# Attention scores from two rounded 32-bit parts on 64 rows, in two row tiles of TensorE side by side, in place of three bf16 parts on 96 rows

## The chip, the cores and the metric

The kernel runs on one core of a Trainium2 chip. A core has TensorE (PE, matmuls into PSUM), VectorE (DVE), ScalarE (ACT), GpSimd (POOL) and SyncE (SP), each with its own queue of instructions, and 16 DMA engines that move data between HBM and the on-chip SBUF. The metric is the device time of one execution in microseconds. Before the change three runs gave 1751.22 to 1751.84 us, with a median of 1751.62 us.

## The reference

The input is x of shape (2, 2048, 256). One transformer layer is computed:

```python
x = x + layernorm(attn(layernorm(x)))
x = x + layernorm(ffn(layernorm(x)))
```

The attention has 16 heads of 16 columns, so with 2 batches there are 32 head units. Its keys and values come from a latent of 64 columns:

```python
q = x @ W_q
latent = (x @ W_k + x @ W_v) @ W_down_kv
k_rec, v_rec = latent @ W_up_k, latent @ W_up_v          # per head
scores = einsum('bhqd,bhkd->bhqk', qh, k_rec) / sqrt(256)
scores = scores * exp(-0.01 * |t_q - t_k|)               # decay, 2048 x 2048
out = softmax(scores) @ v_rec                            # then @ W_o
```

The ffn has 2 shared and 16 routed experts, of which each token uses the best 2. Everything is float32.

## The kernel before, in words

**Stages.** A prologue (`prologue`) normalises x in 8 blocks of 512 tokens, forms the values of all heads, and prepares queries and keys of the first 8 heads of both batches. Then `attention` goes through 32 heads. The ffn follows block by block and is not touched.

**How scores are made.** The decay splits into a factor of the query's place times a factor of the key's place, in two variants (falling, rising) on the two sides of the diagonal. So `prepare` multiplies a projected chunk by both factors. To multiply at float32 accuracy with bf16 operands it splits each product into three bf16 parts (L229 to L235 in the prologue, L527 to L536 in the attention): round, subtract, round the rest, subtract. `store_parts` writes the parts to DRAM (L108). `load_stack` (L111) then gathers, for one head, 96 rows (6 combinations of parts times 16 head columns) for each of four kinds: QL, QU, KL, KU. It issues 12 DMAs for a head: per kind one of 48 rows, one of 32 and one of 16, each row 2048 bf16 numbers or 4 KB. For the queries the 48 and the 32 rows are copies of one part, by a source that repeats (`to_broadcast`). `stack` has two buffers (`par`).

**A head.** It has 16 steps, one for each tile of 128 keys. In step s TensorE makes the scores of 128 keys against 2048 queries in two halves of 1024 (`scores`, L604), each half in 2 or 3 matmuls; ACT takes the exponential of each half in one instruction of 128x1024 (L683); before that DVE multiplies the 128x128 block on the diagonal by a mask (`mask`, L511), which lies in half 0 for s below 8 and in half 1 after that. TensorE then multiplies the probabilities of step s-2 by the values (`products`, L613), four 512-column chunks in four column tiles, in float32. PSUM has three slots of one half each: half h needs the exponential of half h-3 to be done (`halves_done`). In the row of a step the queue of TensorE holds: scores of half 0, products of step s-2, scores of half 1.

**What else rides along.** In the first head of each of the first 12 pairs TensorE projects one chunk of queries and one of keys for later heads (L597, after steps 7 and 11), and DVE prepares them. At step 4 TensorE transposes the sums of the head before (L620).

**The queue of SP.** All DMAs are issued by SP, in program order. While head n runs, SP waits until the scores of head n-1 are done (`sc_ps`), and issues the load of head n+1 into the buffer that became free. In the first head of a pair it then stores the attention output of the pair before (L436), and in the second head, ahead of the load, the four DMAs of freshly prepared parts (L108). Where a load crosses to the next 8 heads it waits until those stores have landed (`out0`, `out1`). TensorE waits at the start of a head for its load (`stk0`, `stk1`).

Of the kernel before, what the change touches and what calls it, by code (L numbers as in the profile page):

```python
# [5 lines left out]
F32 = mybir.dt.float32  # L6
U32 = mybir.dt.uint32
I32 = mybir.dt.int32
BF16 = mybir.dt.bfloat16
ALU = mybir.AluOpType  # L10
# [4 lines left out]
P = 128  # L15
# [20 lines left out]
STACK_DMAS = 12  # L36
BF16_ONES = float(np.array([0x3F803F80], np.uint32).view(np.float32)[0])
PRIME = 2
FLAGS = 936


def emit(nc, io):
    ctx = ExitStack()
    with ctx:
        sb = lambda n, s, d=F32: ctx.enter_context(nc.sbuf_tensor(n, s, d))
        given = []
        def sem(n):
# [9 lines left out]
        w_unit = sb("w_unit", [P, 2, KD, P])  # L57
        stack = sb("stack", [P, 2, 4, S], BF16)
        part = sb("part", [P, 2, 2, 3, CH], BF16)
        work = sb("work", [P, 17408])  # L60
        ps = ctx.enter_context(nc.psum_tensor("ps", [P, 8, CH], F32))

        dram = lambda n, s: nc.dram_tensor(n, s, F32, kind="Internal").ap()
        attn_dram = dram("attn_dram", [T, D])
        parts_dram = nc.dram_tensor("parts_dram", [4, 3, B * H, HD, S], BF16, kind="Internal").ap()

        common = dict(nc=nc, io=io, sem=sem, ident=ident, xT=xT, V_all=V_all, decay=decay, small=small,
                      w_qk=w_qk, w_unit=w_unit, stack=stack, part=part, work=work, ps=ps,
                      attn_dram=attn_dram, parts_dram=parts_dram)
        prologue(**common, shifted=False)  # L70
# [4 lines left out]
        with nc.If(beyond == 1):  # L75
            nc.all_engine_barrier()
            nc.clear_and_free_semaphores(given)
            nc.all_engine_barrier()
            common["sem"] = lambda n: nc.alloc_semaphore("s_" + n)
            prologue(**common, shifted=True)  # L80
            layer(**common, attend=attention_shifted)
# [38 lines left out]
def prologue(nc, io, sem, ident, xT, V_all, decay, small, w_qk, w_unit, stack, part, work, ps, parts_dram, shifted, **_):  # L120
# [36 lines left out]
    with nc.Block() as block:  # L157
# [33 lines left out]
        def _(pool):  # L191
            nc.gpsimd.memset(mhalf, -0.5).then_inc(half_set, 1)
            pool.wait_ge(half_set, 1)
            for n in range(NB):
# [8 lines left out]
                if shifted and n >= NB - 4:  # L203
# [143 lines left out]


def attention(nc, sem, ident, xT, V_all, decay, small, w_qk, w_unit, stack, part, work, ps, attn_dram, parts_dram, first_block, **_):

    probs = carve(work, 0, 3, S)
    Vg = carve(work, 10240, 2, KT, STRIP)
    O_sb = carve(work, 11264, CH)
    att = carve(work, 11776, KT, 2 * HD)
    split = carve(work, 12288, 2, CH)
    dmask, _ = diagonal_masks(small)
    rden = carve(small, 256, CT, QC)
    bound = carve(small, 928, 2)
    bound_new = carve(small, 930, 2)
    bound_all = carve(small, 932, 2)  # L360
    after_bd = carve(small, 934, 1)
    flags = carve(small, FLAGS, B * H // 2 + 1).bitcast(I32)
    QL, QU, KL, KU = range(4)
    ACC = 6

    names = ("vg w proj_ps proj_free prep_link prep_sb sc_ps masked exp_done pv_done o_sb oT_ps rden_sb att_sb").split()
    s_ = {n: sem("a_" + n) for n in names}
    s_.update(att_out=sem("a_att_out"), stk0=sem("a_stk0"), stk1=sem("a_stk1"), out0=sem("a_out0"), out1=sem("a_out1"))
    vg_set, bd_all, bd_link, flag = sem("vg_set"), sem("a_bd_all"), sem("a_bd_link"), sem("a_flag")
    wait = lambda eng, name, v: eng.wait_ge(s_[name], v + PRIME)  # L370
    prime = lambda eng, *ns: [eng.sem_inc(s_[n], PRIME) for n in ns]

    NSTEP = KT
    HALF = S // 2
    NHALF = 2 * NSTEP
    NPAIR = B * H // 2
    PPU = P // HD // 2
    ROWS = 6 * HD
    SCALE = 1.0 / D ** 0.5
    PREPS = 2 * (NPAIR - PPU)  # L380
    chunk = lambda c: slice(c * CH, (c + 1) * CH)

    def cut(lo, hi):

        while lo < hi:
            end = min(hi, (lo // CH + 1) * CH)
            yield lo, end
            lo = end

    def score_pieces(kt, half):  # L390

        a, z = half * HALF, (half + 1) * HALF
        own = kt * P
        for lo, hi in cut(a, min(z, own)):
            yield lo, hi - lo, QU, KU
        for lo, hi in cut(max(a, own), z):
            yield lo, hi - lo, QL, KL

    def half_of(s, half):

        return 2 * ((2 * s + half) % (ACC // 2))

    def halves_done(n, s, half):

        h = 2 * s + half
        return n * NHALF + (h - 1 if h < 2 else h - 2)

    def probs_of(par, s):

        return (par * NSTEP + s) % 3  # L410

    def tiles_done(par, n, s):

        return n * NSTEP + (s - 1 if par == 0 and s < 2 else s - 2)

    def own_block(s):

        at = s * P % HALF
        bank = half_of(s, s * P // HALF) + at // CH
        return ps[:, bank, at % CH:at % CH + P]  # L420

    def pairs(eng, pair):
        pair(0, True, True, False)
        with eng.Fori(1, NPAIR - PPU) as it:
            pair(it, True, False, False)
        with eng.Fori(NPAIR - PPU, NPAIR - 1) as it:
            pair(it, False, False, False)
        pair(NPAIR - 1, False, False, True)

    with nc.Block() as block:  # L430
        @block.sync
        def _(sp):
            def store_att(it):
# [4 lines left out]
            def pair(it, prep, first, last):  # L438
                for par in range(2):
# [6 lines left out]
                    if not end:  # L446

                        wait(sp, "sc_ps", n * NHALF)
                        if not first or par:
                            for which in range(2):  # L450
                                wait(sp, f"out{which}", (it + par) // PPU * (32 * QC))
# [1229 lines left out]
```

## Time and profile before

| | us |
|---|---|
| median of 3 runs | 1751.62 |
| profiled execution, whole | 1757.73 |
| its span, first to last instruction | 1756.0 |
| prologue and first load (to 118) | 118 |
| 32 heads (118 to 1228) | 1110 |
| ffn (1228 to 1756) | 528 |
| PE busy in the span | 1650.1 (94%) |
| ACT busy in the span | 1163.8 (66%) |
| DVE busy in the span | 613.8 (35%) |
| TensorE's granted clock, mean | 0.977 |

The profile is one execution. Its own time, 1757.73 us, is 1.73 us more than its span and 0.35% over the median of the runs. "Busy" counts the time in which at least one instruction of an engine was under way. For matmuls the end of each is modelled, so a busy PE is not a PE at its peak. SP's rows are the issue of DMAs, not their transfer; how busy the DMA engines are is a column of the stage view.

### The profile page before, as it was taken

How to read it: one execution, taken by the hardware profiler on the slowest of the kernel's cores; microseconds unless marked ns; L12 is line 12 of the kernel's file. 1: busy time of each engine (PE TensorE's matmuls, PEld its weight loads, DVE VectorE, ACT ScalarE, POOL GpSimd, SP SyncE). 2: the span in 40 equal slices, each digit the busy share in tenths (PEclk: the TensorE clock that was granted, in tenths of full speed). 3: DMA queues.
4: the chain of work that ended last, by engine and by line, in shares of the span. 5: the costliest groups of instructions: out<-in, count | busy, mean ns of one | idle time of the engine just before them, and what ended most of it. 6: DMA issues, size and time to landing. Idle time of an engine off the chain costs nothing. (4 is left out here: it accounts for less than half of the span.)

```text
span 1756.0 us, 26320 instructions
## 1 busy us (share of the span) xinstructions
PE 1650.1 (94%) x8752; PEld 646.0 (37%) x8753; DVE 613.8 (35%) x1688; ACT 1163.8 (66%) x1330; POOL 59.9 (3%) x104
## 2 busy tenths in 40 slices
PE   7639999999999999999999999998899999999996
PEld 5502222222222222222222222223465565466454
DVE  5804324234143242341341111112344434534432
ACT  4428898988998987989988999998232232222210
POOL 1000000000000000000000000000000000000000
PEclk9969999999999999999999999999899999999998
DMA  7412122122222221222222111123110000100000
GB/s 193 120 64 72 64 76 78 62 75 74 72 74 65 77 73 59 73 79 72 73 62 81 50 44 58 55 87 78 31 37 24 32 16 24 36 12 24 13 12 14
DMA packets 104017, 104.68 MB, mean 60 GB/s; under 512 B 46576, under 2 KB 91376, under 8 KB 103712
## 3 DMA queue, kind: packets, MB, share of 16 engines
q1 hardware_dynamic: 103968, 104.08, 20.2%
q8 instruction: 24, 0.39, 0.1%
q14 instruction: 25, 0.20, 0.0%
HBM read 70.51 MB, written 33.55 MB: 59 GB/s over the span
## 5 line engine op out<-in xcount | busy, mean ns | idle before, releaser
L683 ACT ACTIVATE work<-ps 128x1024 f32<-128x1024 f32 x1024 | 993.9, 1025 | 139.7 <-DVE ps L511 73.4
L604 PE MATMUL ps<-stack 96*128 96x512 bf16 (+3 forms) x2432 | 552.3, 350 | 56.0 <-POOL work L475 32.1
L613 PE MATMUL ps<-work 128*32 128x512 f32 x4096 | 550.6, 610 | 0.0
L511 DVE TENSOR_TENSOR ps<-ps,small 128x128 f32<-128x128 f32 x512 | 153.1, 299 | 804.9 <-PE ps L604 804.9
L604 PEld LDWEIGHTS ps<-stack 96*128 96x128 bf16 x2432 | 189.4, 98 | 620.8 <-ACT work L683 252.2
L1568 PE MATMUL ps<-xT,stack 128*128 (+1 forms) x320 | 156.4, 612 | 1.5 <-PEq L430 1.5
L613 PEld LDWEIGHTS ps<-work 128*32 128x32 f32 x4096 | 81.3, 108 | 189.1 <-ACT work L683 112.0
L1576 PE MATMUL ps<-xT,stack 128*128 (+1 forms) x320 | 150.4, 592 | 0.0
L1591 PE MATMUL ps<-stack,work 128*128 128x256 f32 x640 | 141.3, 380 | 0.0
L1541 ACT ACTIVATE work<-ps 128x512 f32<-128x512 f32 x80 | 47.6, 595 | 135.5 <-PE ps L1568 135.3
L1591 PEld LDWEIGHTS ps<-stack,work 128*128 128x128 f32 x640 | 120.6, 190 | 15.8 <-issue 0.2
L1629 DVE TENSOR_TENSOR work<-work,ps 128x512 f32<-128x512 f32 x80 | 54.9, 687 | 160.0 <-PE ps L1576 152.3
L1576 PEld LDWEIGHTS ps<-xT,stack 128*128 128x128 f32 x320 | 60.9, 190 | 76.8 <-issue 73.0
L1568 PEld LDWEIGHTS ps<-xT,stack 128*128 128x128 f32 x320 | 56.2, 191 | 50.8 <-issue 49.4
L1292 ACT CAST decay<-ps 48x512 f32 (+1 forms) x8 | 4.6, 578 | 80.0 <-PE ps L1329 80.0
L475 POOL COPY work<-V_all 128x256 f32 (+1 forms) x32 | 14.4, 449 | 1014.8 <-PE ps L613 1014.8
L1633 DVE TENSOR_TENSOR work<-work,ps 128x512 f32<-128x512 f32 x64 | 44.0, 687 | 6.7
L597 PE MATMUL ps<-xT,w_unit 128*128 (+1 forms) x96 | 45.2, 592 | 0.0
L304 PE MATMUL ps<-work,xT 128*128 128x256 f32 x128 | 34.7, 420 | 10.9 <-ACT xT L340 10.9
L1285 ACT COPY part<-ps 128x512 f32<-128x512 f32 x16 | 9.4, 585 | 48.2 <-PE ps L1317 48.2
L345 ACT COPY V_all<-ps 128x256 f32<-128x256 f32 x32 | 10.3, 375 | 38.5 <-PE ps L304 38.5
L304 PEld LDWEIGHTS ps<-work,xT 128*128 128x128 f32 x128 | 25.8, 211 | 18.8 <-ACT xT L340 13.4
(119 smaller groups left out, 806.9 us busy)
## 6 DMA issues: line engine op xcount, KB each, us to landing
parts_dram<-part SPq DMA_DIRECT2D x64, 384.0 KB, 4.0
stack<-parts_dram SPq DMA_DIRECT2D x128, 192.0 KB
stack<-parts_dram SPq DMA_DIRECT2D x128, 128.0 KB
work<-in_L_attn_x SPq DMA_DIRECT2D x16, 512.0 KB, 5.0
stack<-parts_dram SPq DMA_DIRECT2D x128, 64.0 KB
attn_dram<-work SPq DMA_DIRECT2D x16, 256.0 KB, 14.0
work<-attn_dram SPq DMA_DIRECT2D x8, 512.0 KB, 3.9
out<-work SPq DMA_DIRECT2D x8, 512.0 KB, 3.0
```

Of the source, the lines that this page charges most:

```text
L304: m = nc.tensor.matmul(ps[:, 6 + j // 2, (j % 2) * D:(j % 2 + 1) * D], xT[:, k, at:at + P], w_veff[:, k], start=k == 0, stop=k == KD - 1)
L511: nc.vector.tensor_tensor(own_block(s), own_block(s), dmask, ALU.mult).then_inc(s_["masked"], 1)
L597: m = nc.tensor.matmul(ps[:, bank], w_unit[:, which, k], xT[:, k, at:at + CH] if isinstance(at, int) else xT[:, k, bass.ds(at, CH)], start ...
L604: m = nc.tensor.matmul(ps[:, half_of(s, half) + q0 // CH % 2, q0 % CH:q0 % CH + w], stack[0:ROWS, par, k, s * P:(s + 1) * P], stack[0:ROWS ...
L613: m = nc.tensor.matmul(ps[STRIP * c:STRIP * (c + 1), ACC + par], Vg[:, par, s], probs[:, probs_of(par, s), chunk(c)], start=s == 0, stop=s ...
L683: nc.scalar.activation(probs[:, probs_of(par, s), half * HALF:(half + 1) * HALF], src, ACT.Exp, scale=SCALE).then_inc(s_["exp_done"], 1)
L1541: nc.scalar.activation(gate[:, h % 2], ps[:, G + h % 2], ACT.Silu).then_inc(s_["gate_sb"], 1)
L1568: m = nc.tensor.matmul(ps[:, G + h % 2], w_up[:, 0, k, h], x(k), start=k == 0, stop=k == KD - 1)
L1576: m = nc.tensor.matmul(ps[:, U + h % 2], w_up[:, 1, k, h], x(k), start=k == 0, stop=k == KD - 1)
L1591: m = nc.tensor.matmul(ps[:, DOWN + j // 2, (j % 2) * D:(j % 2 + 1) * D], hid[:, h, j * P:(j + 1) * P], w_dn[:, h], start=h == 0, stop=h = ...
L1629: nc.vector.tensor_tensor(hid[:, h], gate[:, h % 2], ps[:, U + h % 2], ALU.mult).then_inc(s_["hu_sb"], 1)
L1633: nc.vector.tensor_tensor(hid[:, h], hid[:, h], ps[:, C], ALU.mult).then_inc(s_["h_sb"], 1)
```

## The change

The three bf16 parts become two parts in a 32-bit format that is rounded when it is written (`float32r`). A head then needs 4 combinations of parts times 16 columns, which is 64 rows. The upper 64 rows of SBUF hold the same keys a second time; with them the lower row tile of TensorE (rows 0 to 63) makes the first 1024 queries and the other (rows 64 to 127) makes the last 1024. So keys lie in 128 rows of 2048 numbers and queries in 128 rows of 1024, for the falling and the rising factor each, in 4 bytes a number. The buffers K_st and Q_st lie over `stack` and `work`. `scores` now makes both halves of a step in one go, ahead of the products, with the matmuls of the two tiles in turn. `prepare` has three pieces in place of five. A load is 16 DMAs. `prologue_shifted`, a copy of the old prologue, serves only the path for large scores, which these inputs do not take.

```diff
+def store_halves(sp, halves_dram, part, rows, c, which, done):
+    cols = chunk_at(c)
+    for a in range(2):
+        dst = halves_dram[2 * which + a].rearrange("i h d s -> i (h d) s")[:, rows, cols]
+        sp.dma_start(dst.rearrange("i r s -> r i s"), part[:, which, a]).then_inc(done, 16)
+
+def load_halves(sp, K_st, Q_st, halves_dram, m, par, done):
+    for a in range(2):
+        keys = halves_dram[2 + a].rearrange("i h d s -> i (h d) s")[:, bass.ds(m * HD, HD)]
+        queries = halves_dram[a].rearrange("i h d s -> i (h d) s")[:, bass.ds(m * HD, HD)]
+        for g in range(2):
+            for i in range(2):
+                at = g * TILE_ROWS + 2 * HD * i
+                src = keys[i:i + 1].to_broadcast([2, HD, S])
+                sp.dma_start(K_st[at:at + 2 * HD, par, a, :].bitcast(F32), src).then_inc(done, 16)
+                src = queries[:, :, g * (S // 2):(g + 1) * (S // 2)]
+                sp.dma_start(Q_st[at:at + 2 * HD, par, a, :].bitcast(F32), src).then_inc(done, 16)
...
             for which in range(2):
                 sp.wait_ge(parts_out[which], 2 * 16 * QC)
-            load_stack(sp, stack, parts_dram, 0, 0, stack_in)
+            sp.wait_ge(xn_ready, NB)
+            load_halves(sp, K_st, Q_st, halves_dram, 0, 0, stack_in)
...
-                nc.vector.tensor_copy(pt[:, :, 0], split).then_inc(prep_link, 1)
-                dve.wait_ge(prep_link, 3 * k + 1)
-                nc.vector.tensor_tensor(split, split, pt[:, :, 0], ALU.subtract).then_inc(prep_link, 1)
-                dve.wait_ge(prep_link, 3 * k + 2)
-                nc.vector.tensor_copy(pt[:, :, 1], split).then_inc(prep_link, 1)
-                dve.wait_ge(prep_link, 3 * k + 3)
-                nc.vector.tensor_tensor(pt[:, :, 2], split, pt[:, :, 1], ALU.subtract).then_inc(prep_sb, 1)
+                nc.vector.tensor_copy(pt[:, :, 0].bitcast(F32R), split).then_inc(prep_link, 1)
+                dve.wait_ge(prep_link, k + 1)
+                nc.vector.tensor_tensor(pt[:, :, 1].bitcast(F32R), split, pt[:, :, 0], ALU.subtract).then_inc(prep_sb, 1)
...
-            def scores(par, n, s, half):
-                wait(pe, "exp_done", halves_done(n, s, half))
-                for q0, w, q, k in score_pieces(s, half):
-                    m = nc.tensor.matmul(ps[:, half_of(s, half) + q0 // CH % 2, q0 % CH:q0 % CH + w],
-                                         stack[0:ROWS, par, k, s * P:(s + 1) * P],
-                                         stack[0:ROWS, par, q, q0:q0 + w], start=True, stop=True)
-                m.then_inc(s_["sc_ps"], 1)
+            def scores(par, n, s):
+
+                wait(pe, "exp_done", halves_done(n, s, 1))
+                halves = [list(score_pieces(s, half)) for half in range(2)]
+
+                late = len(halves[0]) > len(halves[1])
+                order = [(0, 0), (1, 0), (0, 1), (0, 2), (1, 1)] if late else [(half, i) for i in range(3) for half in range(2)]
+                for half, i in order:
+                    if i < len(halves[half]):
+                        q0, w, a = halves[half][i]
+                        tile = slice(half * TILE_ROWS, (half + 1) * TILE_ROWS)
+                        m = nc.tensor.matmul(ps[:, half_of(s, half) + q0 // CH % 2, q0 % CH:q0 % CH + w],
+                                             K_st[tile, par, a, s * P:(s + 1) * P], Q_st[tile, par, a, q0 % HALF:q0 % HALF + w],
+                                             start=True, stop=True)
+                        if i == len(halves[half]) - 1:
+                            m.then_inc(s_["sc_ps"], 1)
...
                     for s in range(NSTEP):
-                        scores(par, n, s, 0)
+                        scores(par, n, s)
                         if s >= 2:
                             products(par, n, s - 2)
                         elif not (first and par == 0):
                             products(1 - par, n - 1, NSTEP - 2 + s)
-                        scores(par, n, s, 1)
```

The queue of SP, the load of one head, before (`stack` is the buffer on chip, `parts_dram` the parts in DRAM; a shape is rows by numbers in a row):

```order
L117 DMA stack<-parts_dram 48x1x2048
L117 ISA
L117 DMA stack<-parts_dram 32x1x2048
L117 ISA
L117 DMA stack<-parts_dram 16x2048
L117 ISA
L117 DMA stack<-parts_dram 48x1x2048
L117 ISA
L117 DMA stack<-parts_dram 32x1x2048
```

and after, at the same place:

```order
L149 DMA K_st<-halves_dram 32x1x2048
L151 REGISTER_ALU
L151 DMA Q_st<-halves_dram 32x1x1024
L149 ISA
L149 DMA K_st<-halves_dram 32x1x2048
L151 DMA Q_st<-halves_dram 32x1x1024
L149 DMA K_st<-halves_dram 32x1x2048
L151 ISA
L151 DMA Q_st<-halves_dram 32x1x1024
```

Four groups of 48, 32 and 16 rows of 2-byte numbers became eight pairs of 32 rows and 32 rows of 4-byte numbers.

The queue of TensorE in two steps of a head, before (`a_exp_done` counts the exponentials; `work` holds probabilities and values):

```order
L604 MATMUL ps<-stack 128x512 [waits a_exp_done]
L604 MATMUL ps<-stack 128x512
L613 MATMUL ps<-work 32x512 [waits a_exp_done]
L613 MATMUL ps<-work 32x512 x3
L370 REGISTER_ALU
L604 MATMUL ps<-stack 128x512 [waits a_exp_done]
L604 MATMUL ps<-stack 128x512
L370 REGISTER_ALU
L604 MATMUL ps<-stack 128x512 [waits a_exp_done]
L604 MATMUL ps<-stack 128x512
```

and after:

```order
L627 MATMUL ps<-Q_st,K_st 128x512 [waits a_exp_done]
L627 MATMUL ps<-Q_st,K_st 128x512
L627 MATMUL ps<-Q_st,K_st 128x128
L627 MATMUL ps<-Q_st,K_st 128x384
L627 MATMUL ps<-Q_st,K_st 128x512
L394 REGISTER_ALU
L637 MATMUL ps<-work 32x512 [waits a_exp_done]
L637 MATMUL ps<-work 32x512 x3
```

The two score groups of a step stand together now, behind one wait, and the products stand behind both.

## Rows read from the trace of the kernel before

**Rows 1.** Stages: start:end, us, busy per engine (x), PEclk, DMA share, GB/s
```profile
0.00:118.00 118.00, 63.04 (x241) 44.61 (x243) 64.08 (x150) 36.17 (x83) 12.49 (x28) 0.86 0.48 131
118.00:1228.00 1110.00, 1081.68 (x6772) 307.83 (x6776) 325.53 (x825) 999.63 (x1036) 23.86 (x48) 0.99 0.24 69
1228.00:1756.00 528.00, 505.39 (x1744) 293.54 (x1736) 224.19 (x713) 127.98 (x211) 23.53 (x29) 0.98 0.07 23
```
**Rows 2.** Timeline, two undisturbed steps: start, us, engine, line, what, count
```profile
603.65 1.07 PE L613 MATMUL ps<-work 128*32 128x512 f32 x8
604.65 1.04 PE L604 MATMUL ps<-stack 96*128 96x512 bf16 x5
605.62 1.06 PE L613 MATMUL ps<-work 128*32 128x512 f32 x8
...
605.70 1.94 ACT L683 ACTIVATE work<-ps 128x1024 f32<-128x1024 f32 x2
...
608.41 1.98 ACT L683 ACTIVATE work<-ps 128x1024 f32<-128x1024 f32 x2
```
**Rows 3.** DMA issues of the page: KB each, us to landing
```profile
parts_dram<-part SPq DMA_DIRECT2D x64, 384.0 KB, 4.0
stack<-parts_dram SPq DMA_DIRECT2D x128, 192.0 KB
stack<-parts_dram SPq DMA_DIRECT2D x128, 128.0 KB
...
stack<-parts_dram SPq DMA_DIRECT2D x128, 64.0 KB
```
**Rows 4.** One load of a head: its issue on SP, then stages of 1 us
```profile
1052.31 11.61 SPq L117 DMA_DIRECT2D stack<-parts_dram  x12
...
1061.00:1062.00 1.00, 1.00 (x9) 0.16 (x10) 0.30 (x1) 1.00 (x2) 0.00 (x0) 1.00 0.20 66
1067.00:1068.00 1.00, 1.00 (x11) 0.20 (x9) 0.30 (x1) 1.00 (x2) 0.00 (x0) 1.00 0.13 53
1075.00:1076.00 1.00, 1.00 (x9) 0.16 (x8) 0.10 (x1) 0.97 (x2) 0.00 (x0) 1.00 0.13 53
1076.00:1077.00 1.00, 1.00 (x9) 0.37 (x5) 0.23 (x1) 1.00 (x2) 0.00 (x0) 1.00 0.06 25
```
**Rows 5.** A head whose load came late, on TensorE and ACT, and a stage behind
```profile
672.29 1.03 PE L604 MATMUL ps<-stack 96*128 96x512 bf16 x2 [3.13 <-DMA stack<-parts_dram]
...
675.26 1.96 ACT L683 ACTIVATE work<-ps 128x1024 f32<-128x1024 f32 x2 [4.71 <-PE ps L613]
...
676.00:678.00 2.00, 2.00 (x12) 0.42 (x10) 0.30 (x1) 1.22 (x2) 0.00 (x0) 0.50 0.30 100
```
**Rows 6.** Stages of 1 us: a store of attention output (1034), a store of parts
```profile
1034.00:1035.00 1.00, 1.00 (x9) 0.45 (x11) 0.12 (x1) 0.97 (x2) 0.00 (x0) 1.00 1.02 201
574.00:575.00 1.00, 1.00 (x9) 0.41 (x5) 0.13 (x1) 0.97 (x2) 0.00 (x0) 1.00 1.00 340
```
**Rows 7.** Prologue, its end: the last prepare on DVE, the first loads, TensorE's start
```profile
82.61 0.69 DVE L233 CAST part<-work 128x1024 bf16<-128x1024 f32 x1
83.34 1.23 DVE L235 TENSOR_TENSOR part<-work,part 128x1024 bf16<-128x1024 f32 x1
...
89.51 1.64 SPq L117 DMA_DIRECT2D stack<-parts_dram  x2
...
115.78 2.66 SPq L117 DMA_DIRECT2D stack<-parts_dram  x4
...
117.96 4.23 PE L604 MATMUL ps<-stack 96*128 96x512 bf16 x12 [32.10 <-POOL work L475]
```
**Rows 8.** Timeline, start of the last head on TensorE
```profile
1182.61 0.59 PE L604 MATMUL ps<-stack 96*128 96x512 bf16 x2 [0.49 <-ACT work L683]
```
**Rows 9.** Timeline, a mask on DVE and the exponential that it releases
```profile
1030.94 0.30 DVE L511 TENSOR_TENSOR ps<-ps,small 128x128 f32<-128x128 f32 x1 [2.11 <-PE ps L604]
...
1031.27 1.02 ACT L683 ACTIVATE work<-ps 128x1024 f32<-128x1024 f32 x1 [0.18 <-DVE ps L511]
```

More of the change, by code:

```diff
@@ L9 @@
 BF16 = mybir.dt.bfloat16
+F32R = mybir.dt.float32r
 ALU = mybir.AluOpType
@@ L36 @@
 STACK_DMAS = 12
+TILE_ROWS = 4 * HD
+HALVES_DMAS = 16
 BF16_ONES = float(np.array([0x3F803F80], np.uint32).view(np.float32)[0])
@@ L39, with aligned @@
 FLAGS = 936
+def aligned(at):
+    return (at + 31) // 32 * 32
 def emit(nc, io):
@@ L57, in emit @@
         w_unit = sb("w_unit", [P, 2, KD, P])
+        stack_at = aligned(nc.sbuf_base)
         stack = sb("stack", [P, 2, 4, S], BF16)
         part = sb("part", [P, 2, 2, 3, CH], BF16)
+        work_at = aligned(nc.sbuf_base)
         work = sb("work", [P, 17408])
+        K_st = nc.alloc_sbuf_tensor_at("K_st", [P, 2, 2, S], F32R, offset=stack_at)
+        Q_st = nc.alloc_sbuf_tensor_at("Q_st", [P, 2, 2, S // 2], F32R, offset=work_at + 4 * 3 * S)
         ps = ctx.enter_context(nc.psum_tensor("ps", [P, 8, CH], F32))
@@ L64, in emit @@
         attn_dram = dram("attn_dram", [T, D])
+        halves_dram = nc.dram_tensor("halves_dram", [4, 2, B * H, HD, S], F32, kind="Internal").ap()
         parts_dram = nc.dram_tensor("parts_dram", [4, 3, B * H, HD, S], BF16, kind="Internal").ap()
@@ L68, in emit @@
                       w_qk=w_qk, w_unit=w_unit, stack=stack, part=part, work=work, ps=ps,
-                      attn_dram=attn_dram, parts_dram=parts_dram)
-        prologue(**common, shifted=False)
+                      attn_dram=attn_dram, parts_dram=parts_dram, halves_dram=halves_dram, K_st=K_st, Q_st=Q_st)
+        prologue(**common)
         layer(**common, attend=attention)
@@ L79, in emit @@
             common["sem"] = lambda n: nc.alloc_semaphore("s_" + n)
-            prologue(**common, shifted=True)
+            prologue_shifted(**common)
             layer(**common, attend=attention_shifted)
@@ L117, in load_stack @@
             sp.dma_start(stack[row * HD:(row + count) * HD, par, kind, :], parts).then_inc(done, 16)
-def prologue(nc, io, sem, ident, xT, V_all, decay, small, w_qk, w_unit, stack, part, work, ps, parts_dram, shifted, **_):
+def store_halves(sp, halves_dram, part, rows, c, which, done):
[3 more added lines that the diff above has]
+        sp.dma_start(dst.rearrange("i r s -> r i s"), part[:, which, a]).then_inc(done, 16)
@@ L122, in prologue, with prologue_shifted @@
+def prologue_shifted(nc, io, sem, ident, xT, V_all, decay, small, w_qk, w_unit, stack, part, work, ps, parts_dram, **_):
     w_k = carve(work, 0, KD, D)
@@ L201, in _ @@
                     nc.gpsimd.tensor_copy(w_unit[:, :, :, :], w_qk[:, :, :, 0:P]).then_inc(w_set, 1)
-                if shifted and n >= NB - 4:
+                if n >= NB - 4:
                     if n == NB - 4:
```

783 lines of the change are left out of this document (486 added, 297 removed).

## The prediction

> **What bounds the kernel now.** I read the stages first, then the timeline of single steps, then the DMA part of the page, and last one load of a head in stages of 1 us. The 32 heads take 1110 of 1756 us, with TensorE busy for 1082 of them; the ffn takes 528 and is left as it is [rows 1]. In an undisturbed step TensorE goes from products (603.65) to scores (604.65) to the next products (605.62): 1.00 + 0.97 = 1.97 us, without a gap. ACT's exponentials start every (608.41 - 605.70) / 3 = 0.90 us there, so its floor is 1.81 us a step [rows 2]. TensorE sets the pace, by 0.16 us a step. That is what one sees first, and it says that cheaper scores can win at most 512 x 0.16 = 82 us.
>
> The column that matters for this change is another one. Over the heads the 16 DMA engines are 0.24 busy [rows 1], which looks like ample room. But the load of one head, issued at 1052.31, still runs at 1076: 24 us for 1.57 MB, out of the 34.6 us that a head takes (1110 / 32). From 1067 on the share is 0.13 at 53 GB/s, and 0.13 x 16 is 2 engines; before that, at 1061, it is 0.20, 3 engines [rows 4]. So the load goes over two or three engines, one after another. The bytes agree. If a DMA of 48 rows is cut over 3 engines, one of 32 rows over 2 and one of 16 rows over 16, and each takes the same first engines, then these carry, of the 192, 128 and 64 KB per kind [rows 3], 64 + 64 + 4 = 132 KB, times four kinds 528 KB, or 541 thousand bytes. At 53 / 2.08 = 25.5 GB/s an engine that is 21 us; seen are 24.2 us from the issue to the end, with about 2 us ahead of the first data. Had each DMA gone to engines of its own, five would have been busy at once.
>
> The Trainium skill, "DMA: Bandwidth & Descriptors", section "Why a DMA increments its semaphore by 16 and not by 1", states this as a rule: a DMA runs on the largest number up to 16 that divides the slowest dimension of both sides, and on the lowest-numbered engines. By that rule the 48-row DMAs (a source that leads with 3) get 3 engines and the 32-row ones (a source that leads with 2) get 2, which the trace bears out, and each of the 16 new DMAs would get 2.
>
> **The change part by part.** *The load.* Every new DMA has 32 rows on chip and a source that leads with 2 (two copies, or two parts), like the old 32-row ones; none is left of 48 or 16 rows. Keys are 128 rows x 2 x 2048 x 4 = 2.10 MB and queries 128 x 2 x 1024 x 4 = 1.05 MB: 3.15 MB in place of 1.57. All of it goes over 2 engines, 1.573 million bytes each, in place of 0.541: 2.9 times as much on the busiest. At the tail's 25.5 GB/s a load takes 61.7 us. At the rate of a whole load of before, 0.541 / 24.2 = 22.3 GB/s with its start counted, 70.4 us. I take 64: back to back there is no start to pay, but at 1061 three engines moved 66 GB/s, only 20.6 each, in the part with repeated sources [rows 4], and keys are such a part.
>
> *Where it lies.* 64 us is longer than a head. Load n+2 may be issued when head n's scores are done, some 35 us after load n landed, while load n+1 still has 29 us to go. So the two engines have the next load queued always, and the period of a head is their load time. Double buffering hides a head behind a load now, not a load behind a head.
>
> *The sum.* Prologue: each of 8 prepares on DVE loses one cast (0.69 us) and one subtraction (1.23) [rows 7], about 15 us if the first copy keeps its 0.69, 11 if it rises to 1.2 by writing four bytes; I take 12. The added wait on xn_ready is for ACT's work that was long done. So the first load is issued at 89.5 - 12 = 77.5. Before, the next load was issued 26.3 us after it (115.78 - 89.51); now 26.3 + (64 - 22.3) = 68 later, at 145.5, with data from 147.5. Then:
> - 31 loads x 64 = 1984;
> - stores of parts in 12 pairs: 4 x 524 KB, 131 KB on each engine, at 340 / 16 = 21 GB/s [rows 6] 6.2 us; before, one landed in 4.0 us [rows 3]; I take 5.5, 66 us in all;
> - 14 stores of attention output ahead of the last load, in pieces of 128 bytes: 16 KB an engine at 201 / 16.3 = 12.3 GB/s [rows 6] is 1.3 us; I take 2.5 for the small pieces, 35 in all (18 to 55);
> - 3 crossings to the next 8 heads, where the load waits for stores to land: 4 us each, 12.
>
> The last load has landed at 147.5 + 1984 + 66 + 35 + 12 = 2244.5. From there on the kernel ends as now: the last head started at 1182.6 [rows 8], 573.4 us before the end of the span. TensorE comes cold out of its wait: after such a wait of 3.13 us the granted clock was 0.50 (1.2 GHz) and still stood there at 676, and ACT had lost 4.7 us by 675.26 [rows 5]; I add 5. Span 2823, execution 2825 with the 1.7 us around it; the median stood 0.35% under the profiled execution, which gives 2815. I forecast 2815.
>
> *Scores and products.* They lie beneath the loads and cost nothing as long as a head stays under 64 us. The exponential (1.02), the scores, the mask (0.30) and some 0.1 of hand-overs [rows 9] form a chain in steps 0 to 7, since half 0 of a step now waits, with half 1 behind the same wait, for the exponential of half 0 of the step before. The trace has no matmul in the rounded format. Lower bound of a score stage: half of today's 0.97, two tiles at bf16's speed, 0.49 us. Upper bound: float32 products take 1.00 us for four chunks side by side [rows 2], so four score matmuls of that price one after another 4.0 us. A head is then 16 x 1.9 = 31 us at the low end and 16 x (4.0 + 1.02 + 0.4) = 87 at the high one; in pairs, 16 x 3.4 = 55. I take the low end, nearest to the bf16 row in work; only the high end would show. The wait for `halves_done(n, s, 1)` at step 0 asks for the last exponential of the head before: about 1.2 us a head, hidden too. If the loads were hidden, all this would count.
>
> *DVE.* Two operations less per prepare, in slack before and after. The store is ready earlier, but queued behind a load.
>
> **The rivals.** A: the new DMAs spread over all engines. For it: stores and ffn weights do (340 GB/s, share 1.00 [rows 6]); at that rate a load takes 9 us. Then heads run at their own pace: steps 0 to 7 at 1.02 + 0.65 + 0.4 = 2.07 us, the others at ACT's 1.81, and 1.2 at the start, 32.3 against 16 x 1.97 = 31.5 now: +26 us; the prologue gives 12 and the late loads [rows 5] some 15. About 1750: this is the side of faster or no change. Against it: 32-row DMAs ran at share 0.13 [rows 4]. The section "Bandwidth" of the same page of the Trainium skill speaks for A, since larger transfers move faster there (64 KB at 138 GB/s, 1 MB at 341), and ours grow from 64 to 192 KB to 128 and 256 KB; but the rows have 53 GB/s for 128 and 192 KB, and the measurement decides.
> B: the scores cost the high end, 87 us a head, and set the pace themselves: 147 + 32 x 87 + 528 = 3460. It decides from 64 us a head, that is a score stage of some 2.6 us. Nothing in the trace speaks for float32's price, since each score is still one matmul in the queue, but a float32 product is one there too and shows as two rows.
> C: the two engines run dry between loads, because SP is held back in its issues (12 took 11.6 us [rows 4]) or by its waits: 4 to 8 us a load more, 2940 to 3060.
>
> **How the numbers follow.** The forecast has 86%; A 4% (half of it faster), B 3%, C 7%. Its own bounds: 61.7 us a load and the low ends of the stores give 2815 - 74 - 35 = 2705, somewhat less if rows of 8 KB run better than those of 4 KB; 70.4 gives 3020. My range is 2670 to 2990. A measurement of this kernel can tell 0.2% from no change: faster 0.03, same 0.01, slower 0.96.
>
> **What would show it.** Right: a DMA share of 0.13 nearly throughout the heads at 50 to 53 GB/s; starts of heads 64 to 67 us apart; about 28 us in each in which TensorE waits for K_st or Q_st; a granted clock that falls to 0.50 in each wait. Wrong: a share of more than 0.25 during a load, or heads under 60 us apart (then the two engines are not the limit), or TensorE busy throughout heads of 80 us and more (B).

## The result: 2738.9 us in place of 1751.7

Four runs of the changed kernel gave 2735.64 to 2742.2 us with a median of 2738.88; four of the kernel before gave 1751.22 to 1754.92 with a median of 1751.73. The ratio is 1.563, with a 95% interval of 1.560 to 1.566. The forecast was 2815 us in a range of 2670 to 2990: the direction, the mechanism and the range held, and the time came out 76 us (2.7%) under the forecast.

The stages of the profile after (columns as in [rows 1]):

```profile
0.00:66.00 66.00, 49.95 (x176) 33.47 (x177) 38.15 (x118) 26.43 (x60) 10.59 (x22) 0.97 0.74 182
66.00:2190.00 2124.00, 1051.87 (x6749) 359.78 (x6750) 288.99 (x763) 971.88 (x1041) 22.13 (x50) 0.75 0.20 65
2190.00:2740.00 550.00, 521.71 (x1828) 301.01 (x1828) 231.97 (x744) 143.10 (x231) 25.87 (x32) 0.97 0.08 25
```

Nearly all of the loss is in the heads: the first one starts at 152.7 us where it started at 118.0, which is 35 us of the 987, and from there on no engine does more work than before. In the second stage TensorE is busy for 1052 of 2124 us, the granted clock averages 0.75, and the 16 DMA engines are 0.20 busy at 65 GB/s. That looks like an idle machine; what binds it is hidden by the average over 16 DMA engines. The wait table (engine, line, releaser: us in total, times, longest) names what the machine waits for:

```profile
PE ps L627 <- DMA Q_st<-halves_dram: 879.2, 31, 41.1
```

31 waits, one for each head after the first, 28.4 us on average. The starts of three heads in TensorE's timeline (start, duration, in brackets the idle time ahead of it and what ended it), and the stages of one load between them:

```profile
1530.44 0.79 PE L627 MATMUL ps<-Q_st,K_st 64*128 64x512 f32 x2 [19.15 <-DMA Q_st<-halves_dram]
...
1602.18 1.22 PE L627 MATMUL ps<-Q_st,K_st 64*128 64x512 f32 x4 [38.16 <-DMA Q_st<-halves_dram]
...
1662.15 1.22 PE L627 MATMUL ps<-Q_st,K_st 64*128 64x512 f32 x4 [21.76 <-DMA Q_st<-halves_dram]
```

```profile
1615.00:1625.00 10.00, 9.10 (x63) 3.47 (x59) 1.70 (x6) 7.86 (x9) 0.00 (x0) 1.00 0.13 52
...
1655.00:1662.00 7.00, 0.00 (x0) 0.00 (x0) 0.00 (x0) 0.00 (x0) 0.00 (x0) 0.50 0.13 49
1664.00:1666.00 2.00, 2.00 (x13) 0.71 (x5) 0.00 (x0) 1.68 (x2) 0.00 (x0) 0.50 1.09 208
1666.00:1672.00 6.00, 5.30 (x37) 1.40 (x34) 1.49 (x4) 4.45 (x5) 0.40 (x1) 0.90 0.99 185
```

A load without stores beside it takes 1662.15 - 1602.18 = 60.0 us at share 0.13, which is 2 engines of 16: the rows of the old late load [rows 4], now from end to end. 3.15 MB / 2 / 60.0 us is 26.2 GB/s an engine. Where stores of parts come between two loads, the period is 71.7 us: at 1664 all 16 engines are busy, at only 208 / 16 = 13 GB/s each. (The share adds up the times of the packets, so it can pass 1.) TensorE's granted clock is 0.50 (1.2 GHz) in the wait, still 0.50 at 1664, two us into the next head, and 0.90 on average from 1666 to 1672.

The steady steps of a head, which [rows 2] showed for before:

```profile
1877.93 0.74 PE L627 MATMUL ps<-Q_st,K_st 64*128 64x512 f32 x5 [0.45 <-ACT work L706]
1878.60 0.16 PEld L637 LDWEIGHTS ps<-work 128*32 128x32 f32 x8
1878.60 1.07 PE L637 MATMUL ps<-work 128*32 128x512 f32 x8
1878.71 0.30 DVE L534 TENSOR_TENSOR ps<-ps,small 128x128 f32<-128x128 f32 x1 [1.26 <-PE ps L627]
1879.05 1.94 ACT L706 ACTIVATE work<-ps 128x1024 f32<-128x1024 f32 x2 [0.25 <-DVE ps L534]
1880.12 0.53 PEld L627 LDWEIGHTS ps<-Q_st,K_st 64*128 64x128 f32 x5 [1.36 <-ACT work L706]
1880.12 0.73 PE L627 MATMUL ps<-Q_st,K_st 64*128 64x512 f32 x5 [0.45 <-ACT work L706]
```

The score stage fell from 0.97 to 0.67 us (1877.93 to 1878.60), so the rounded parts on two row tiles do make scores cheaper. Yet the step is 1880.12 - 1877.93 = 2.19 us, longer than the 1.97 of before: TensorE now idles 0.45 us for ACT, and ACT 0.25 us for the mask. From step 8 on a step takes 1.84 us (1889.67 to 1891.52).

### The profile page after: what moved, and what is told of

Same layout as the page of the kernel before. It is cut to its first block and busy times, and to the rows that moved or that the text cites. A ratio compares the mean times of both kernels' runs of the same rounds, so it can differ in the third digit from the quotient of the medians.

```text
span 2740.4 us, 26402 instructions
## 1 busy us (share of the span) xinstructions
PE 1623.5 (59%) x8752; PEld 694.3 (25%) x8753; DVE 559.1 (20%) x1624; ACT 1141.4 (42%) x1330; POOL 58.6 (2%) x104
## 5 line engine op out<-in xcount | busy, mean ns | idle before, releaser
L706 ACT ACTIVATE work<-ps 128x1024 f32<-128x1024 f32 x1024 | 971.4, 1022 | 1138.1 <-PE ps L637 607.2
L627 PE MATMUL ps<-Q_st,K_st 64*128 64x512 f32 (+3 forms) x2432 | 423.4, 437 | 1066.9 <-DMA Q_st<-halves_dram 879.2
L627 PEld LDWEIGHTS ps<-Q_st,K_st 64*128 64x128 f32 x2432 | 234.3, 203 | 1556.7 <-issue 916.9
L637 PE MATMUL ps<-work 128*32 128x512 f32 x4096 | 598.2, 659 | 0.0
L1569 PE MATMUL ps<-w_qk,work 128*128 128x256 f32 x128 | 31.9, 392 | 0.0
```

What stands on the lines that cost most here:

```text
L627: m = nc.tensor.matmul(ps[:, half_of(s, half) + q0 // CH % 2, q0 % CH:q0 % CH + w], K_st[tile, par, a, s * P:(s + 1) * P], Q_st[tile, par, ...
L637: m = nc.tensor.matmul(ps[STRIP * c:STRIP * (c + 1), ACC + par], Vg[:, par, s], probs[:, probs_of(par, s), chunk(c)], start=s == 0, stop=s ...
L706: nc.scalar.activation(probs[:, probs_of(par, s), half * HALF:(half + 1) * HALF], src, ACT.Exp, scale=SCALE).then_inc(s_["exp_done"], 1)
L1569: m = nc.tensor.matmul(bank[:, j * D:(j + 1) * D], aT[:, k, at:at + P], w_o[:, k], start=k == 0, stop=k == KD - 1)
```

## The experiments

Each edit is against the kernel named. Unless said otherwise a kernel had 4 runs, timed beside the kernel before on the same chip; intervals in square brackets are 95%, the others go from the lowest to the highest run.

**1. The new scores, with loads over all engines (`spread`).** Each DMA of 32 rows becomes two of 16 rows, without a leading 2 in the source.

```diff
-                src = keys[i:i + 1].to_broadcast([2, HD, S])
-                sp.dma_start(K_st[at:at + 2 * HD, par, a, :].bitcast(F32), src).then_inc(done, 16)
-                src = queries[:, :, g * (S // 2):(g + 1) * (S // 2)]
-                sp.dma_start(Q_st[at:at + 2 * HD, par, a, :].bitcast(F32), src).then_inc(done, 16)
+                for j in range(2):
+                    lo = at + j * HD
+                    sp.dma_start(K_st[lo:lo + HD, par, a, :].bitcast(F32), keys[i:i + 1]).then_inc(done, 16)
+                    src = queries[j:j + 1, :, g * (S // 2):(g + 1) * (S // 2)]
+                    sp.dma_start(Q_st[lo:lo + HD, par, a, :].bitcast(F32), src).then_inc(done, 16)
```

> The changed kernel with every load of 32 rows cut into two of 16 rows (source and chip both lead with 16), the same bytes. Theory, two engines carry the load: each new DMA takes all 16 engines, a load lasts some 20 to 22 us (now bound by SP's issues, 32 x 0.6 us), less than a head, and TensorE no longer waits for Q_st. A head then runs at its own pace as the trace of the changed kernel shows it, 33.4 us, 36 with the projections: 111 + 12 x 71.5 + 4 x 67 + 527 + some 13 = 1777 us, 1755 to 1795. Rival 1, the bytes themselves are too many (3.15 MB a head, any layout): time stays over 2500. Rival 2, the rounded matmuls or the row tiles are slow: TensorE busy throughout and over 2000.

Measured: 1787.66 us (1786.84 to 1789.31), 1.019 times before [1.016, 1.022]. The same bytes, twice as many DMAs, and 951 us are gone; TensorE has no wait for a load. So the two engines are the cause of all the loss but 36 us. The stage of the heads in this kernel, and the start of a pair's first head on ACT:

```profile
66.00:1200.00 1134.00, 933.72 (x6510) 324.14 (x6508) 280.88 (x738) 936.13 (x1000) 22.03 (x50) 0.98 0.86 118
```

```profile
903.13 1.94 ACT L707 ACTIVATE work<-ps 128x1024 f32<-128x1024 f32 x2 [1.85 <-PE ps L638]
906.06 1.94 ACT L707 ACTIVATE work<-ps 128x1024 f32<-128x1024 f32 x2 [0.98 <-PE ps L638]
```

Now neither TensorE nor ACT is the bound (934 and 936 of 1134 us). What is left is waits between them. And the DMA engines are 0.86 busy for only 118 GB/s, 8.6 GB/s an engine.

**2. The same cut in the kernel before (`before_spread`).** 48-row and 32-row DMAs become 3 and 2 of 16 rows.

> The kernel before, with its loads of 48 and 32 rows cut into DMAs of 16 rows (24 for a head in place of 12). Theory: its loads go from 24 us to under 18, the three late ones (some 5 us of ACT each) no longer are late, and the first load in the prologue shrinks from 22 us to some 14: 1752 - 15 - 8 = 1729, 1722 to 1740. Rival: its late loads come from the wait on stores and not from two engines: 1744 or more. Beside the run named spread it says what the rounded parts and row tiles cost or win by themselves.

Measured: 1732.36 us (1729.58 to 1733.43), 0.987 of before [0.985, 0.990], as forecast. The old layout suffered a little from the same cause: TensorE's 7 waits for a load (12.5 us in all, and not 3, as I had counted) are gone, and the first head starts at 106.31 and not at 117.96. At equal spreading the change itself costs 1787.7 - 1732.4 = 55 us (3.2%), though it shortens TensorE's work (the score stage from 0.97 to 0.67 us). About 10 of the 55 lie ahead of the heads, whose first starts at 115.87 in `spread`; some 46 lie in the heads.

**3. Two thirds of the bytes (`keys_only`).** Queries are loaded for the first two heads only, and later heads reuse them, so its output differs. One run.

> The changed kernel with the queries loaded for the first two heads only (later heads use stale queries, so the output differs): the same two engines, 2.10 MB a load in place of 3.15. Theory: the period is bytes over the rate of two engines, 52.4 GB/s, so 60.0 becomes 40.0 us: 2739 - 30 x 20 = 2139, with the first heads at 60 and stores now partly beside a load; 2120 to 2200, as heads with projections take 41 us. Rival, a fixed cost for each DMA (8 in place of 16): the same direction, but then the period would not be two thirds; a fixed cost alone gives 30 us or the head's own 35, some 1990.

Measured: 2134.5 us, one run. Head starts:

```profile
1178.33 1.22 PE L628 MATMUL ps<-Q_st,K_st 64*128 64x512 f32 x4 [17.00 <-DMA K_st<-halves_dram]
1218.09 0.73 PE L628 MATMUL ps<-Q_st,K_st 64*128 64x512 f32 x4 [1.54 <-DMA K_st<-halves_dram]
```

39.8 us for 2.10 MB is 26.4 GB/s on each of two engines. These are all sources that repeat. Half as many DMAs took two thirds of the time, so the rival of a fixed cost for each DMA falls. Time follows the bytes on an engine, and a repeated source is no slower than another, against what I had read into the row of 1061 [rows 4].

**4. The pitch of the array in DRAM (`after_pad`).** The changed kernel, rows 8.5 KB apart; a load reads the first 2048 numbers of each row.

```diff
-        halves_dram = nc.dram_tensor("halves_dram", [4, 2, B * H, HD, S], F32, kind="Internal").ap()
+        halves_dram = nc.dram_tensor("halves_dram", [4, 2, B * H, HD, S + PAD], F32, kind="Internal").ap()
```

> The changed kernel with its 16 DMAs a head, only the array of halves in DRAM made 2176 values wide (rows 8.5 KB apart). My prediction put 5.5 us on the stores of parts in each load that has them; the trace shows 9.7 (71.7 us from one load's end to the next, and 62.2 where there are only attention stores). Theory: the 8 KB pitch slows the stores, 512 KB at about 200 GB/s. With 8.5 KB they take 5 to 6 us, the loads stay at 60.0 us (26.2 GB/s on each of two engines), and 12 x 4 = 48 us and 3 us in the prologue go: 2739 becomes 2685 to 2695. Rival: the stores are slow for their runs of 2 KB; nothing changes, 2735 to 2740. A time below 2650 would mean that the pitch also set the 60.0 us.

Measured: 2681.24 us (2678.81 to 2681.96), 58 less, a little more than forecast. The end of a load with stores and of one without:

```profile
1609.54 1.22 PE L628 MATMUL ps<-Q_st,K_st 64*128 64x512 f32 x4 [20.42 <-DMA Q_st<-halves_dram]
...
1679.18 1.22 PE L628 MATMUL ps<-Q_st,K_st 64*128 64x512 f32 x4 [35.82 <-DMA Q_st<-halves_dram]
...
1739.21 1.22 PE L628 MATMUL ps<-Q_st,K_st 64*128 64x512 f32 x4 [23.60 <-DMA Q_st<-halves_dram]
```

The load stays at 60.0 us. The period of a load with stores is 67.4 us as a rule (this one crosses to new heads, 69.6), in place of 71.7, and 62.1 with an attention store alone in both kernels: the stores of parts cost 5.3 us, not 9.6. The second head starts 6.9 us earlier (206.51, not 213.39), since prologue stores land sooner: DVE waited for them for 5.9 us, not 12.1. The 8 KB pitch was the cause of the slow stores, and not of the 60.0. One thing does not fit: the first pair, which has no attention store beside its stores, takes 65.6 us with either pitch. Why the pitch costs nothing there was not tried.

**5. The same pitch where loads are spread (`spread_pad`, on 1).**

> The kernel with 32 DMAs of 16 rows a head, its DRAM array of halves made 2176 instead of 2048 values wide, so that rows stand 8.5 KB apart and not 8 KB. In the run with 8 KB the DMA engines are busy for 0.89 of the attention stage and move only 121 GB/s (7.5 GB/s an engine; the kernel before moves 75 GB/s at a share of 0.29, 16 GB/s an engine). Theory: the engines read at addresses a multiple of 8 KB apart at the same time and meet in the memory. Then the share falls to 0.3 to 0.5 at about the same 120 GB/s, and the stores of 512 KB (8.5 us to land) land in 4 to 6. Since TensorE waits for no load there, the time stays near 1788, 1780 to 1790. Rival: the pitch does not matter (the source rows are read twice, or the SBUF side limits): share 0.85 to 0.9 as before, 1788.

Measured: 1779.93 us (1779.51 to 1781.63), 8 less than 1: the first head starts at 107.74 and not at 115.87. The stages from 200 to 1000, of 1 first and of this kernel second:

```profile
200.00:1000.00 800.00, 681.22 (x4766) 231.03 (x4767) 216.60 (x560) 682.14 (x721) 14.96 (x32) 1.00 0.88 121
```

```profile
200.00:1000.00 800.00, 680.84 (x4768) 230.51 (x4766) 216.16 (x558) 682.67 (x720) 15.03 (x32) 1.00 0.82 120
```

The share fell from 0.88 to 0.82, not to the 0.3 to 0.5 that I expected. The pitch explains the stores and a little of the loads. What holds spread loads at 121 / 16 / 0.88 = 8.6 GB/s an engine stays open (the 7.5 of the expectation leaves the share out). One hint is in the first load of each kernel, when the other engines are nearly idle: DMAs of 16 rows moved 114 to 140 GB/s in `spread` (90 to 110 us, share 0.93 to 1.17) and 131 to 148 in `before_spread` (92 to 102 us, share 0.45 to 0.58). The totals are much closer than the rates an engine, so the limit may lie in something that all DMAs of 16 rows share. No run loads with larger DMAs that go over all engines.

**6. The half without the diagonal first (`spread_turn`, on 1).** ACT and the order of the matmuls take the half that needs no mask first.

```diff
+    def turn(s, half):
+        return half if s * P // HALF else 1 - half
...
-                        for half in range(2):
+                        own = s * P // HALF
+                        for half in (1 - own, own):
```

> As spread, and in each step ACT takes the half without the diagonal first, so that the mask on DVE lies beside an exponential. Theory: steps 0 to 7 fall from 2.18 to the 1.84 us of the other steps, 8 x 0.34 x 32 = 87 us less than spread, some 1690 (1670 to 1710). Rival, the chain of steps 0 to 7 is held by the score matmuls and not by the mask: less than 30 us.

Measured: 1736.99 us (1735.38 to 1743.92); 51 gained, not 87. ACT's waits for the mask in 1, and for the scores in this kernel (the longest of each is the one for the first load):

```profile
ACT work L707 <- DVE ps L535: 109.9, 228, 29.2
```

```profile
ACT work L711 <- PE ps L632: 99.3, 79, 30.8
```

The mask was a cause: without the first one, 80.7 us of waits for it went. But waits for the scores, 35.9 us in 1, rose to 68.5. The forecast took 0.34 us off eight steps of each head; in the trace of a pair's first head steps 2, 3, 4, 6 and 7 lost their idle time of 0.23 to 0.29 us on ACT, while 1.85 and 0.98 us at a pair's start and 0.31 at step 5 stayed, and step 8 of a head with projections idled 1.64 us in place of 1.30. The rest was given back by loads: TensorE waited for one three times, 9.1 us in all, and the clock fell with it.

```profile
939.29 1.22 PE L632 MATMUL ps<-Q_st,K_st 64*128 64x512 f32 x4 [3.20 <-DMA Q_st<-halves_dram]
```

```profile
930.00:940.00 10.00, 6.51 (x51) 2.43 (x43) 0.90 (x3) 7.05 (x8) 0.00 (x0) 0.91 1.06 123
940.00:950.00 10.00, 7.71 (x38) 2.04 (x34) 1.44 (x4) 4.76 (x5) 0.40 (x1) 0.50 1.08 125
```

**7 and 8. An earlier first step of a head, without and with the pitch (`spread_turn_first` on 6, `spread_turn_first_pad`).** At step 0 each half's scores have their own wait.

```diff
-                wait(pe, "exp_done", halves_done(n, s, 1))
+                if s:
+                    wait(pe, "exp_done", halves_done(n, s, 1))
...
+                    if s == 0 and i == 0:
+                        wait(pe, "exp_done", halves_done(n, 0, 1 - half))
```

> The kernel with 32 DMAs a head and the half without diagonal taken first, where at a head's first step the second half's scores wait only for their own banks (order of that step: both pieces of the second half, then both of the first). Theory: the joint wait holds ScalarE at each head's start (1.85 and 0.98 us in the run with 32 DMAs, 0.9 with the turn): 31 x 1.0 to 1.2 us go, 1737 becomes 1700 to 1706. Rival: the scores of the first half come later since the two row tiles do not run side by side in that step; the head start keeps its price and the time stays at 1733 to 1740.

> The same with rows 8.5 KB apart in DRAM. Theory of the pitch: the late load at a crossing (TensorE waits 3.2 us at 939 in the run with the turn and runs to 948 at 1.2 GHz, about 5 us lost at each of up to three crossings) goes as well: 1688 to 1698. Rival: the pitch does not matter: the same time as the kernel without it.

Measured: 1741.51 us (1733.36 to 1742.0) without the pitch, 1719.25 (1717.99 to 1722.27) with it. The first is a miss, no faster than 6, and late loads are not the reason: TensorE waited 5 times for one, 9.9 us in all, where it was 3 times and 9.1 us in 6. What the edit changed is the start of a pair's second head, where ACT's idle 0.90 us became 0.14 and 0.37. With the pitch one wait of 0.7 us is left and the first head starts 9 us earlier, and 22 us are gained, more than the 5 us at each of three crossings that were forecast for the pitch. The time missed its 1688 to 1698 all the same, since these were counted from a gain that the first edit did not bring. The idle times of 1.85 and 0.98 us at the start of a pair's first head still stood on ACT:

```profile
1051.53 1.94 ACT L717 ACTIVATE work<-ps 128x1024 f32<-128x1024 f32 x2 [1.85 <-PE ps L648]
1054.44 7.48 ACT L717 ACTIVATE work<-ps 128x1024 f32<-128x1024 f32 x8 [0.98 <-PE ps L648]
```

They end with products (L648), not with scores. The buffers of exponentials rotate by three, and 32 steps of a pair are not a multiple of three. So the first exponential of a pair overwrites a tile whose products are queued behind the joint scores.

**9. A fourth buffer of exponentials (`four_buffers`, on 8).** It lies where the bf16 parts lay; the last head of all keeps to three.

```diff
+    def probs(last, par, s, cols):
+        i = s % 3 if last and par else s % 4
+        return fourth[:, cols] if i == 3 else three[:, i, cols]
```

> The best kernel so far (32 DMAs, turned halves, separate waits at a head's first step, rows 8.5 KB apart: 1719.25) with a fourth buffer for the exponentials, in the array of bf16 parts that this kernel no longer fills; the last head keeps three. Theory: at every second head's start ScalarE idles 1.85 and 0.98 us because its third-last buffer is still to be read by the products queued behind the joint scores; with four buffers this goes: 15 x 2.8 = 42 us, 1674 to 1685, unless loads come late again (then up to 1700). Rival: the stall is due to the scores' own banks and stays: 1715 to 1720.

Measured: 1679.87 us (1678.63 to 1680.61), 0.957 of before [0.955, 0.958], and 39 less than 8. The forecast of 42 came from the two idle times, and they are gone. A pair starts at 951.35:

```profile
949.43 1.94 ACT L720 ACTIVATE part<-ps 128x1024 f32<-128x1024 f32 x2
951.35 2.19 ACT L720 ACTIVATE work<-ps 128x1024 f32<-128x1024 f32 x2
953.85 3.86 ACT L720 ACTIVATE work<-ps 128x1024 f32<-128x1024 f32 x4 [0.30 <-PE ps L641]
```

**10 to 12. The halves apart (`spread_apart` on 5, `apart_four`, `apart_turn_four` on 9).** Scores of one half, products, scores of the other, each half with its own wait, as in the kernel before.

```diff
-                wait(pe, "exp_done", halves_done(n, s, 1))
+                wait(pe, "exp_done", halves_done(n, s, only))
...
-                        scores(par, n, s)
+                        scores(par, n, s, 0)
                         if s >= 2:
                             products(par, n, s - 2)
...
+                        scores(par, n, s, 1)
```

> The kernel with 32 DMAs of 16 rows a head and rows 8.5 KB apart (1779.93 measured), with the halves' scores again in two stretches: first half, products, second half, each with its own wait as in the kernel before; the operands stay in 64 rows and the two row tiles never run side by side. The steady score stage of both halves side by side takes 0.69 us there. Theory that running side by side is what makes it cheap: each half alone takes as long as both, 0.6 to 0.7, so TensorE needs 2 x 0.65 + 1.06 + 0.2 = 2.6 us a step, and 512 steps make it 1980 to 2050. Rival, which holds that the joint wait costs more than the pairing saves: a half alone takes 0.3 to 0.4, TensorE is free again before ScalarE (1.87 us a step), and the time falls to the 1720 to 1745 of the kernel before with 24 DMAs (1732).

Measured: 1731.15 us (1728.78 to 1732.29), 49 less than 5 at equal loads. The time was the rival's, but its reason was not. One half alone and both halves, in this kernel:

```profile
877.04 0.73 PE L627 MATMUL ps<-Q_st,K_st 64*128 64x512 f32 x2
877.70 1.06 PE L637 MATMUL ps<-work 128*32 128x512 f32 x8
878.70 0.74 PE L627 MATMUL ps<-Q_st,K_st 64*128 64x512 f32 x4
879.36 1.06 PE L637 MATMUL ps<-work 128*32 128x512 f32 x8
880.36 1.24 PE L627 MATMUL ps<-Q_st,K_st 64*128 64x128 f32 x5
881.53 1.06 PE L637 MATMUL ps<-work 128*32 128x512 f32 x8
```

Two matmuls of one half take 0.66 us (877.04 to 877.70), four of both halves 0.66 too: the row tiles do run side by side, and a half alone costs as much as both, as the first theory had it. What that theory did not see is that in this order too a step's second half and the next step's first half are neighbours in TensorE's queue, and run side by side without a common wait. They do it less well, 0.66 to 1.17 us a stage against 0.66 to 0.72 with the matmuls in turn, but TensorE has that time: a step took 1.83 us from 1003.69 to 1005.52. What ACT waited for, in 5 and then in this kernel (the longest wait for the mask is again the first load):

```profile
ACT work L708 <- DVE ps L536: 107.8, 228, 27.0
ACT work L708 <- PE ps L639: 42.8, 30, 2.0
```

```profile
ACT work L707 <- DVE ps L536: 70.7, 75, 25.6
ACT work L707 <- PE ps L637: 11.7, 15, 0.9
```

Waits for the mask fell by 36 us and those for products by 31; those for scores rose by 11 (35.8 to 46.8). The joint wait bought TensorE time that nobody needed, and cost 49 us.

> The kernel with the halves' scores apart (1731.15) with four buffers for the exponentials. The pairs' starts cost ScalarE 0.78 us there on products (11.7 us in all) and 0.44 us on the masked block. Theory: only the 11.7 us go, since with the halves apart products are queued behind one half's scores alone: 1715 to 1722. Rival: four buffers are worth what they were in the paired kernel (39 us): 1690 to 1695.

Measured: 1726.67 us (1724.9 to 1731.04), 4.5 less than `spread_apart` and 5 over the forecast range. The runs of the two kernels overlap, so 4.5 is not clear of noise. Four buffers are worth 39 us only where products stand behind both halves' scores.

> The kernel with four buffers and turned halves (1679.87), its halves' scores apart instead of side by side: first the half without the diagonal, then products, then the half with it, each behind its own wait. Theory: side by side buys nothing, since a half alone takes about 0.35 us, and the joint wait costs; ScalarE is idle 59 us between 107 and 1100 in the paired kernel, in steps of 0.3 us, and most of this goes: 1650 to 1670. Rival: once the order of the halves is turned the pairing pays, since TensorE switches row tiles once a step and not twice: 1680 to 1700.

Measured: 1759.81 us (1756.15 to 1761.72, 10 runs), 80 more than 9: a miss on both sides. ACT's waits, of this kernel first and of 9 second, between 107 and 1150 us:

```profile
ACT work L715 <- DVE ps L543: 84.3, 101, 1.9
```

```profile
ACT work L720 <- DVE ps L543: 2.4, 5, 1.7
```

With the masked half's scores made last, behind the products, the mask is the last link more often: in 512 steps ACT waited 101 times for it. In 9 both halves are made before ACT begins, and the mask is done while ACT works on the other half. So neither order is better by itself: the turned halves want joint scores (1680 against 1760, four buffers), the plain ones scores apart (1731 against 1780, three buffers).

## Why the prediction was right, point by point

- **Two engines carry each load.** Right, and shown by experiment 1 (spread: the loss goes), 3 (bytes: 39.8 and 60.0 us at the same 26.2 to 26.4 GB/s an engine) and the share of 0.13 throughout. The prediction read it off the old loads [rows 4]. The rule that it set beside them, from the Trainium skill, "DMA: Bandwidth & Descriptors", section "Why a DMA increments its semaphore by 16 and not by 1" (the largest number up to 16 that divides the slowest dimension of both sides), is borne out by the traces for `to_broadcast` sources and for two-part sources alike, at share 0.13. The same page's section "Bandwidth" of the Trainium skill, by which larger transfers move faster (measured there on DMAs issued by GpSimd), did not decide here: DMAs of 128 and 256 KB on two engines moved 52 GB/s, DMAs of 64 and 128 KB cut for sixteen 121.
- **The period of a head is its load.** Right. The next load was always queued: the period is 60.0 us to 0.1, and the engines never ran dry (rival C). The signs came as named, a share of 0.13, waits of 28.4 us and a clock of 0.50 in each, but for one: starts of heads 60.0 us apart lie outside the named 64 to 67 and on the edge of "under 60", which was to speak against two engines. That edge was set too near. Experiment 3, with starts 39.8 apart, is what shows that the two engines are the limit.
- **64 us a load.** Mis-sized: 60.0, so 31 x 4 = 124 us too much. The step that failed is the reading of 20.6 GB/s an engine at 1061 [rows 4] as a price of repeated sources. Keys alone ran at 26.4 (experiment 3). The low bound of 61.7, from the tail's 25.5, was the nearer, and it too was 2.8% high.
- **Stores of parts, 5.5 us.** Mis-sized the other way: 9.6 (71.7 - 62.1) in 11 pairs and 5.6 in the first, 111 us in place of 66. With rows 8.5 KB apart they cost 5.3 (experiment 4); the 340 GB/s of [rows 6] came from rows that stood otherwise.
- **Attention stores 2.5, crossings 4.** Measured 2.1 (62.1 - 60.0) and 2.8 (74.5 - 71.7): 6 and 4 us too much in the sums.
- **Prologue saves 12 us.** It saved 2.6: the first load was issued at 86.86, not 77.5. DVE did lose its two operations a prepare, but waited 12.1 us, 4 times, for stores that had not landed (1.2 us, once, before). The prediction had no term for stores that grew from 384 to 512 KB. From there to the next issue it took 63.7 us, not 68, so the second load was issued 5 us late (150.53 against 145.5).
- **The end after the last load, 578.4.** Measured 2740.4 - 2162.8 = 577.6.
- **The sum.** 2823 + 5 - 124 + 45 - 6 - 4 - 1 = 2738; the span is 2740.4. That the forecast came within 2.7% is in part luck: without the 45 us that the stores cost more, the load's error alone would have put it 121 us off.
- **Scores at the low end, and hidden.** Right: 0.67 us a stage where 0.49 was the bound, and a head computes for about 33.4 us of its 60. Rivals A and B fell with the share of 0.13 and the idle TensorE. The price that A gave for hidden loads, +26 us in the heads, was too low: of the 55 us between `spread` and the old scores with spread loads some 46 lie in the heads. A step took 2.19, not 2.07, and a pair's first head had the 2.8 us on the rotating buffers, which the prediction had not seen.

## What to carry to other kernels

Count DMA engines per transfer, not bytes alone: a mean share of 0.13 of 16 engines may be two engines at their limit, and cutting along the slow dimension so that every transfer uses all engines was worth 951 us here and some 20 in the old kernel. Before cheaper matmuls are paid for with a common wait, see what stands behind that wait in the queue (a mask, products, a rotating buffer), and whether the old order does not put the same matmuls side by side already. With spread loads, turned halves, an earlier first step, padded rows and a fourth buffer the new scores do win: 1679.87 us, 4.3% under the kernel before and 3.0% under the old scores with spread loads. Whether turned halves or a fourth buffer would also speed up the old scores was not run.

## What the runs showed of the hardware that I had not expected

- One DMA engine moved 26.2 GB/s in 60 us without a break when two were at work, but 8.6 GB/s when all 16 read rows of 4 and 8 KB at once (`spread`: 121 GB/s at share 0.88; not explained); in the old kernel with spread loads, 72 GB/s at share 0.28, it was 16.
- Stores of 512 KB landed in 8.5 us (median) at an 8 KB pitch and in 4.6 at 8.5 KB, with the same runs of 2 KB (experiment 4).
- SP's issue of a DMA took 0.6 to 0.8 us for the first six of a load on two engines, and 7.0 us for the ninth; the longest issue of a load in the run took 17.9 us. In `spread`, over 16 engines, the DMAs of the first load took 0.3 to 0.4 us each:

```profile
90.45 0.64 SPq L151 DMA_DIRECT2D Q_st<-halves_dram  x1
...
94.95 7.02 SPq L149 DMA_DIRECT2D K_st<-halves_dram  x1
```

- Two matmuls of 64x512 in the rounded format take 0.66 us in one row tile, and four over both row tiles take 0.66 too. In `spread_apart` the two tiles overlapped wherever their matmuls were neighbours in the queue, fully at 878.70, in part at 880.36, where five with as many columns as four of 512 took 1.17 us in place of 4 x 0.33 = 1.32.
